# Node projection of a graph layer: the transposes of two feature slices are issued together

## The reference, cut to what matters

```python
x = _layernorm(x)                          # (10000, 1024)
x = x * rsqrt(mean(x * x) + EPS) * rms_w
x = x @ W_down                             # 1024 -> 256
xl = x @ Wl                                # 256 -> 256
xr = x @ Wr                                # 256 -> 256
```

## Time and profile before

| | us |
|---|---|
| median of 3 runs | 2142.32 (2140.77 to 2144.11) |
| profiled execution, its own time | 2144.25 |
| its span, first to last instruction | 2142.5 |
| TensorE busy | 1946.7 (91% of the span) |
| DVE, ACT, POOL busy | 1072.7, 717.4, 394.9 |
| mean granted TensorE clock | 0.971 of full speed |

### The profile page before, as it was taken

One profiled execution on the slowest core, in us unless ns is written; L12 is line 12 of the kernel. 1 busy time (PEld: TensorE's weight loads), 2 busy tenths in 40 slices (PEclk: granted clock), 3 DMA queues, 4 the chain that ended last, 5 costly groups with the idle time before them and its releaser, 6 DMA issues.

```text
span 2142.5 us, 26616 instructions
## 1 busy us (share of the span) xinstructions
PE 1946.7 (91%) x8982; PEld 1535.9 (72%) x8982; DVE 1072.7 (50%) x1990; ACT 717.4 (33%) x1161; POOL 394.9 (18%) x389
## 2 busy tenths in 40 slices
PE   4999999946562899999999999999999999999998
PEld 3888888822232777787778777877787778777876
DVE  6666666526563545434543454345434544454443
ACT  3555555413270233223322332233223322332232
POOL 2121121158601111011101110111011101111000
PEclk9999999978986899999999999999999999999999
DMA  7556656264423220222022202220222022202211
GB/s 189 140 142 160 164 137 159 59 173 116 138 63 117 72 87 25 63 87 87 23 63 86 86 21 65 86 86 19 67 86 86 17 69 86 86 14 72 77 39 39
DMA packets 78718, 184.81 MB, mean 86 GB/s; under 512 B 38743, under 2 KB 46045, under 8 KB 73801
## 3 DMA queue, kind: packets, MB, share of 16 engines
q1 hardware_dynamic: 49811, 137.91, 22.1%
q0 software_dynamic: 25632, 25.89, 4.8%
q10 hardware_dynamic: 3234, 20.48, 3.9%
HBM read 117.36 MB, written 66.62 MB: 86 GB/s over the span
## 4 chain that ended last, share of the span: by engine, by line
PE 80%; DMA 4%; issue 4%; DVE 4%; POOL 3%; ACT 2%; SPq 1%; ACTq 0%; DVEq 0%; POOLq 0%
PE psum L1244 22%; PE psum L1246 22%; PE psum L1245 22%; PE psum L1389 3%; PE psum L1268 3%; PE psum L1441 2%; PE psum L1443 2%; POOL xls L501 2%; POOL td L505 1%; DMA td<-node_table,dst_idx 1%; PE psum L1490 1%; ACT xld L654 1%; PE psum L1322 1%; SPq L374 1%; PE psum L1476 1%
## 5 line engine op out<-in xcount | busy, mean ns | idle before, releaser
L675 ACT ACTIVATE cxt_hi<-psum 128x500 fp32r<-128x500 f32 x160 | 94.1, 588 | 579.4 <-PE psum L1389 579.4
L1244 PE MATMUL psum<-w_hi,h_hi 128*125 128x512 f32 x640 | 254.6, 398 | 21.1 <-DVE h_lo L1092 21.1
L1244 PE MATMUL psum<-cxt_hi,w_hi 128*128 128x500 f32 x640 | 259.9, 406 | 0.6 <-DVE cxt_lo L1063 0.6
L1245 PE MATMUL psum<-w_lo,h_hi 128*125 128x512 f32 x640 | 251.9, 394 | 0.0
L1246 PE MATMUL psum<-w_hi,h_lo 128*125 128x512 f32 x640 | 251.5, 393 | 0.0
L1245 PE MATMUL psum<-cxt_lo,w_hi 128*128 128x500 f32 x640 | 249.5, 390 | 0.0
L1246 PE MATMUL psum<-cxt_hi,w_lo 128*128 128x500 f32 x640 | 249.3, 390 | 0.0
L554 POOL TENSOR_TENSOR h_lo<-gl,h_hi 128x500 fp32r<-128x500 f32 x60 | 78.8, 1338 | 839.1 <-ACT h_hi L683 839.1
L1073 DVE TENSOR_TENSOR cx<-cx,psum 125x512 f32<-125x512 f32 x160 | 109.2, 682 | 239.0 <-PE psum L1246 238.9
L1063 DVE TENSOR_TENSOR cxt_lo<-psum,cxt_hi 128x500 fp32r<-128x500 f32 x160 | 107.6, 673 | 215.0 <-ACT cxt_hi L675 215.0
L1142 DVE TENSOR_TENSOR cx<-cx,psum 125x512 f32<-125x512 f32 x160 | 103.4, 684 | 111.2 <-PE psum L1246 111.2
(11 more groups left out here) (209 smaller groups left out, 3650.1 us busy)
## 6 DMA issues: line engine op xcount, KB each, us to landing
cx<-in_x SPq DMA_DIRECT2D x80, 448.0 KB
out<-cx SPq DMA_DIRECT2D x80, 448.0 KB
ax<-in_x SPq DMA_DIRECT2D x19, 1792.0 KB
node_table<-trow ACTq DMA_DIRECT2D x19, 896.0 KB
node_table<-xld SPq DMA_DIRECT2D x10, 500.0 KB
cx<-in_x SPq DMA_DIRECT2D x80, 52.0 KB
out<-cx SPq DMA_DIRECT2D x80, 52.0 KB
ax<-in_x SPq DMA_DIRECT2D x19, 208.0 KB
```

Of the source, the lines that this page charges most:

```text
L675: act.activation(cxt_hi[:, k % 2, :], T_C[k % 2][:, 0:G], ACT.Copy).then_inc(c_hi, 1)
L1244: pe.matmul(out_ap, left[0], right[0], start=start, stop=False, skip_group_check=True)
L1245: pe.matmul(out_ap, left[0], right[1], start=False, stop=False, skip_group_check=True)
```

## The change

In stage A the turns are issued in pairs. Within a group, turns k + 2 and k + 3 now stand together ahead of product k for k = 0, 2 and 4, where before turn k + 2 stood ahead of each product k. At the end of a group, T0' and T1' stand together behind LR1, where before T0' stood behind LR0 and T1' behind LR1. Nothing else is changed; the semaphores and their counts are the same.

```diff
             def body(g, par):
                 for k in range(KD):
-                    if k + 2 < KD:
+                    if k % 2 == 0 and k + 2 < KD:
                         turn(g, par, k + 2)
+                        turn(g, par, k + 3)
                     pe.wait_ge(a_lo, KD * g + k + 1)
...
                 for j in range(J):
                     if has(g, -1):
                         left_right(g - 1, 1 - par, j)
-                    if j < 2 and has(g, 1):
-                        turn(g + 1, 1 - par, j)
+                    if j == 1 and has(g, 1):
+                        turn(g + 1, 1 - par, 0)
+                        turn(g + 1, 1 - par, 1)
```

## The result

The changed kernel takes 2151.68 us (median of 12 runs, 2147.33 to 2155.46). The kernel before took 2143.67 us beside it (12 runs). The ratio is 1.0038, with a 95% interval of 1.0027 to 1.0049: 8 us slower (5.8 to 10.5), where 9.5 us was forecast. The profiled execution took 2153.95 us, against 2153.8 us in the forecast.

A forecast was written before the change was run, and what follows sets the result against it. TensorE's instruction order was taken to bound steady stage A. Switches and moves among products counted nothing; 18 stalls of 0.53 us added 9.5 us to 2142.32, giving a median of 2151.8 us, range 2147 to 2155.5.

The forecast's parts named there:

- A switch costs nothing that matters: TensorE, stage A: removing 78 switches between transposes and products gains 0.00 us each, bounded by 0.8 us either way in total.
- What moves among the products: Stage A, within a group: turns moved one product earlier add no wait for `low`; cost nothing.
- Start-up: First two groups of stage A: the moved turn falls into TensorE's idle time waiting for DVE; taken as nothing.
- The chain from T0' to LR3: End of groups 1 to 18: T0', high0', low0', copy of LR1, LR3 take 3.01 us; 0.53 us stall each, 9.5 us.
- The new line of waits: Sign in the profile after: TensorE's L1244 waits for DVE's `trow` L864, 18 times, 0.4 to 0.5 us each.
- stages B and C were to differ by no more than 1 us: Sign: a difference of more than 1 us in stages B or C would make the prediction wrong.
- The switch price: Rival, TensorE: each of 78 switches has its own price, giving back up to 8.6 us, 2143.2 us in all; chance 0.05.
- the copy comes in time: Rival, end of group: ACT or DVE releases earlier, LR3 does not wait, time stays 2142.3 us; chance 0.05.
- a second wait: Rival, stage A: late low1' holds product 1 or the next group's normalization, 2155 to 2165 us; chance 0.04.
- The clock did not fall: Rival, TensorE in stage A: joined transposes or the stall drop the clock, 65 us more, past 2200 us; chance 0.03.

The follow-up runs named there:

- The pairs alone: Kernel before with only turns k + 2 and k + 3 paired ahead of product k, end of group unchanged: ratio 0.9987, then 1.0002 the second time.
- Taking transposes apart: Kernel before with each transpose of turns 3 to 7 alone between two matmuls of product k - 3: 2147.26 us against 2141.96, ratio 1.0022.
- the copy first: Changed kernel with DVE's copy of LR1 moved ahead of low0': 2143.0 us against 2143.33 for the kernel before, ratio 1.0003.
- the pair behind LR0: Changed kernel with T0' and T1' together one left-right product earlier, behind LR0 instead of LR1: ratio 1.0004 to the kernel before.
- the pair behind LR2: Changed kernel with T0' and T1' together one left-right product later, behind LR2 instead of LR1: 2175.64 us in 2 runs, ratio 1.0145 to before.

## Why the prediction was right

**A switch costs nothing that matters.** This holds. Eight transposes joined take 1.02 us, and from their start to the second matmul behind them it is 1.09 us (208.78 to 209.87), the distance of the earlier trace rows. The pairs alone change a group by 0.014 us. Taking transposes apart bounds the price of a switch at 0.01 us in the groups, the bound that the prediction had set for it. The 0.47 us of the first matmul behind a turn is reported 15 times more in each of those groups, which are 0.151 us longer and not 15 x 0.08, so it is no price of a switch. That it is an exposed weight load is the reading of the earlier trace rows; no run separates the load from the rest of a transpose.

**What moves among the products is free.** This holds: no wait of any product for `low` in the steady groups, in either kernel. Start-up, taken at nothing too, was 2.0 us shorter in the profile.

**The chain from T0' to LR3.** Predicted 3.01 us, measured 2.98 to 3.00 us in 14 of the 18 groups and 2.91 or 2.92 us in the other four. The terms were 0.71, 0.62, 0.60, 0.74 and 0.34; measured were 0.71, 0.62, 0.60, 0.73 and 0.33. The four are groups 1, 2, 3 and 18, and the difference is in the first link: ACT starts 0.63 us after T0' there. They are the groups that ACT's program has written out, while groups 4 to 17 run in its loop (`Fori`). The prediction took its rows from a group in the loop. The stall was forecast at 0.53 us a group, and a group grew by 0.505. Over 18 groups that is 9.1 us instead of 9.5: the chain is 2.97 us on average, 0.04 less than predicted. That the chain is the cause was shown by moving its start both ways and by taking the copy out of it.

**What was off.** The new line of waits was forecast as 18 waits of 0.4 to 0.5 us each by the reported start. It reads 3.6 us for 16 of them, 0.2 us each. The step had set the first start of LR3 against the start that it would have had (by that measure it is 0.38 us late on average), while the profile counts only from the modelled end of the matmul ahead, 0.17 us later. And stages B and C were to differ by no more than 1 us, or the prediction was wrong; they differ by 2.5 us in the two profiles. That sign was badly chosen, since stage B alone differs by 2.7 us between two profiles of the kernel before and by 10 us over the kernels.

**What was luck.** The mechanism and its size are shown in the groups, but the two times come out closer than the sum deserves. The profiled execution is 0.15 us from its forecast because 9.1 us in the groups, 2.0 us less in start-up and 2.5 us more in stages B and C add up to 9.7 (rounded values). The median is 0.1 us from its forecast because the loss was smaller than forecast (8.0 against 9.5 us) and the kernel before, with 12 runs instead of 3, stood at 2143.67 us instead of 2142.32.

**The rivals.** The switch price fell with the transposes taken apart, "the copy comes in time" with the 18 waits of the weight loads in the trace, and a second wait did not appear. The clock did not fall: 1.00 from 62 to 420 us with four runs of eight transposes in each group. The Trainium skill's sentence that the full clock does not engage on transposes ("TensorE: Matmul & The Clock Gate", "Part 4: PE-mode transpose") gave no danger for such runs between products. In the changed kernel a run of 27 transposes, some of them small, from 46.40 to 49.12 us had a granted clock of 1.00 too. The 16 that open the program (19.39 to 22.62 us, behind 19 us of idle) stand 0.20 us apart instead of 0.107, though the profile gives 1.00 for them as well; no run separates the idle time from the transposes there.

No version beat the kernel before in a way that came back. With the copy first, or with the pair behind LR0, the paired turns are as fast as the single ones.

## What to carry to other kernels

Before joining instructions to save switches, look in the trace at what the first instruction behind a switch waits for: here the weight loads pointed to one load for each transpose, in any order, and a joined run elsewhere in the same trace had the price ready. Moving an instruction later on the engine that sets the time costs nothing there, but it is the head of a chain over other engines, and their queues are in order: count from it through everything queued behind its consumer, back to the first instruction that waits. If such a chain is too long by a little, turn the order on the engine in the middle, so that the release that the bound engine needs does not stand behind work that needs the late input.

## What was not expected of the hardware

A wait of TensorE is worth more than the profile's waits say: 0.505 us a group in distances between starts against 0.2 us reported. The matmul ahead is reported 0.17 us longer than the distance to the next, and the second matmul behind the wait follows after 0.33 us instead of 0.23. With the pair behind LR2 it is 1.90 us against 1.6.

The same hand-over from TensorE to ACT, on the same instructions, took 0.71 us in the groups of ACT's loop and 0.63 us in those written out (0.77 and 0.69 us in the kernel before). Why was not tested.

One kernel measured against itself over 12 and 23 runs gave 1.0004 (0.9992 to 1.0016), and the pairs among the products, with a stage A as long as before, gave 0.9987 (0.9975 to 0.9999) once and 1.0002 the second time. Stage B, which gathers rows by index, spread from 250.9 to 260.7 us over ten profiles, while a steady group of stage A repeated to 0.001 us in two profiles of the same kernel. For an effect of this size the period of a group says more than the time of the kernel.
